# Attention stage of a one-core transformer block: VectorE takes the maximum of the new scores ahead of the low part of the turned tile

## What is computed

```python
q = rope(x @ w_q); k = rope(x @ w_k); v = x @ w_v            # 32, 8, 8 heads
lk = rope((x @ w_lq) @ w_lk); lv = x @ w_lv                  # 32 heads
attn = causal_softmax(q k^T / sqrt(128)) v                    # k, v repeated 4 times
lat  = causal_softmax(q lk^T / sqrt(128)) lv
x = layernorm(x + attn @ w_o + lat @ w_lo)
x = layernorm(x + top1_lora_ffn(x))                           # 8 experts of rank 16
```

## Time and profile before

| | us |
|---|---|
| median of 3 runs | 2026.87 |
| lowest, highest | 2025.49, 2027.67 |
| the profiled execution, its own time | 2023.68 |
| its span, first to last instruction | 2021.7 |
| TensorE busy in it | 1979.0 |
| VectorE busy in it | 1356.1 |
| ScalarE busy in it | 1054.6 |
| GpSimd busy in it | 1129.1 |

### The profile page before, as it was taken

The page is one execution under the profiler, slowest core; times in us unless marked ns, Lnnn a source line. Parts: engine busy times, 40 slices in busy tenths (PEclk is TensorE's granted clock), DMA queues, the critical chain, the costliest instruction groups (busy, mean ns, idle before and its releaser), DMA issues.

```text
span 2021.7 us, 39463 instructions
## 1 busy us (share of the span) xinstructions
PE 1979.0 (98%) x12640; PEld 1806.8 (89%) x12640; DVE 1356.1 (67%) x3356; ACT 1054.6 (52%) x2445; POOL 1129.1 (56%) x905
## 2 busy tenths in 40 slices
PE   7999999999999999999999999999999999999994
PEld 6989989899898989989899898999989899898993
DVE  6758667585775747758476675757757586675756
ACT  3746627375372745728356372654727366272641
POOL 6637476374664647556465664646566374763730
PEclk9999999999999999999999999999999999999997
DMA  5010010101000010000100001010010100100001
GB/s 177 12 35 1 23 36 12 35 1 43 15 22 24 2 57 1 22 24 3 55 1 22 24 22 36 1 45 1 23 36 12 35 1 23 36 13 21 2 12 42
DMA packets 19366, 50.85 MB, mean 25 GB/s; under 512 B 5824, under 2 KB 7872, under 8 KB 19008
## 3 DMA queue, kind: packets, MB, share of 16 engines
q1 hardware_dynamic: 18992, 45.90, 6.8%
q10 hardware_dynamic: 144, 2.10, 0.2%
HBM read 45.89 MB, written 2.10 MB: 24 GB/s over the span
## 4 chain that ended last, share of the span: by engine, by line
PE 97%; DVE 1%; issue 1%; POOL 0%; DVEq 0%; POOLq 0%; ACT 0%; ACTq 0%
PE ps L349 28%; PE ps L350 28%; PE ps L351 28%; PE ps L435 13%; DVE stats L845 0%; PE ps L529 0%; PE ps L544 0%; PE ps L521 0%; DVE acc L870 0%; POOL pt_lo L688 0%; DVE acc L908 0%; DVE stats L844 0%; POOL mask L678 0%; DVE neg_max L782 0%; DVE acc L831 0%
## 5 line engine op out<-in xcount | busy, mean ns | idle before, releaser
L712 POOL TENSOR_TENSOR probs<-probs,inv_sum 128x640 f32<-128x640 f32 (+7 forms) x512 | 582.9, 1150 | 343.9 <-DVE inv_sum L789 342.9
L782 DVE CUSTOM_DVE_ANT_0 probs<-ps,mask 128x640 f32<-128x640 f32 (+7 forms) x512 | 384.3, 753 | 167.2 <-PE ps L351 121.1
L724 DVE TENSOR_TENSOR pt_lo<-ps,pt_hi 128x512 fp32r<-128x512 f32 (+3 forms) x768 | 399.0, 547 | 75.1 <-ACT pt_hi L551 73.2
L551 ACT ACTIVATE pt_hi<-ps 128x512 fp32r<-128x512 f32 (+3 forms) x768 | 347.0, 487 | 164.0 <-PE ps L435 160.8
L580 ACT ACTIVATE probs<-probs,neg_max 128x640 f32<-128x640 f32 (+7 forms) x512 | 397.0, 776 | 60.5 <-DVE neg_max L782 49.3
L349 PE MATMUL ps<-pt_hi,val_hi 128*128 128x256 f32 x1216 | 353.8, 291 | 0.0
L350 PE MATMUL ps<-pt_lo,val_hi 128*128 128x256 f32 x1216 | 342.7, 282 | 0.0
L351 PE MATMUL ps<-pt_hi,val_lo 128*128 128x256 f32 x1216 | 342.5, 282 | 0.0
L435 PE MATMUL ps<-ident,probs 128*128 128x128 f32 x2304 | 334.4, 273 | 0.0
L703 POOL TENSOR_TENSOR probs<-probs 128x512 f32<-128x512 f32 x144 | 186.7, 1296 | 198.9 <-DVE probs L758 198.9
L435 PEld LDWEIGHTS ps<-ident,probs 128*128 128x128 f32 x2304 | 271.9, 140 | 23.6
(11 more groups left out here) (100 smaller groups left out, 4025.6 us busy)
## 6 DMA issues: line engine op xcount, KB each, us to landing
raw<-wo SPq DMA_DIRECT2D x32, 512.0 KB, 3.4
raw<-wq SPq DMA_DIRECT2D x16, 512.0 KB, 3.8
raw<-wlv SPq DMA_DIRECT2D x16, 512.0 KB, 3.6
raw<-wkv SPq DMA_DIRECT2D x8, 512.0 KB, 3.6
acc<-xT SPq DMA_DIRECT2D x4, 512.0 KB, 6.2
wlk_raw<-wlk SPq DMA_DIRECT2D x16, 128.0 KB, 3.0
acc<-x ACTq DMA_DIRECT2D x1, 2048.0 KB, 8.8
out<-acc SPq DMA_DIRECT2D x8, 256.0 KB, 2.4
```

Source lines behind the costliest of these rows:

```text
L551: return nc.scalar.activation(dst, src, ACT.Copy)
L712: nc.gpsimd.tensor_tensor(b, b, inv_sum[:, k % 8:k % 8 + 1].to_broadcast([P, b.shape[-1]]), ALU.mult).then_inc(q["normed"], 1)
L724: return nc.vector.tensor_tensor(dst, src, h, ALU.subtract)
L782: nc.vector.tensor_tensor_reduce(out=probs_of(n).rearrange("p (b n) -> p b n", b=b), in0=scores_of(n), in1=mask[:, S - w:S].rearrange("p ( ...
```

## The change

In the slot loop of VectorE's program two steps change places: `row_max` of tile k now comes ahead of `probs_lo` of tile k-5. Nothing else is changed.

```diff
                     for k in range(SLOTS):
+                        if EARLY + MID <= k < TILES:
+                            row_max(g, pair, k)
                         if 0 <= k - LO_LAG < TILES:
                             probs_lo(g, pair, k - LO_LAG)
-                        if EARLY + MID <= k < TILES:
-                            row_max(g, pair, k)
                         if EARLY <= k - 1 < TILES:
                             inverse(g, pair, k - 1)
```

## The result

The changed kernel takes 2109.4 us (median of 4 runs, 2106.1 to 2110.15) against 2026.4 (2025.49 to 2027.67): slower by 83 us, a ratio of 1.0406 with a 95% interval of 1.0388 to 1.0424. Forecast were 2117 and a range of 2080 to 2175. One run of the first experiment with four banks and the change took 2400.27 us at a granted clock of 0.788, and no figure here includes it.

A forecast was written before the change was run, and what follows sets the result against it. The prediction took TensorE, without idle time in the slots, to bound the kernel. Turn waits of 5.66 us a pair, times 16 = 91 us, on 2023.7 gave 2114, plus 3.2 for the median 2117; range 2080 to 2175.

The forecast's parts named there:

- TensorE has nothing to give back, the margin is what counts: In the slots TensorE is busy 60.57 of 60.60 us, so any wait is added in full, 16 times.
- The mechanism: TensorE's turns wait for banks held by later low parts: +91 us, 82 in 100.
- Slots 24 and 30: Even slots with long distances between turns: loss 0, at most 0.1 us.
- The sum, slot by slot: Turn waits in named slots add without growing: 5.66 us a pair, times 16 = 91 us.
- slots 22 and 23: Turns lose 0.18 us in slot 22 and 0.50 in slot 23, where VectorE is late after a short product.
- slots 31 and 32: At the pair's end, without scores between two turns, the second unit starts 1.38 us later.
- Earlier maxima gain nothing: TensorE's waits for maxima precede the exchanged steps: gain taken as 0, bounded by 8.7 us.
- Other work queued behind the maximum costs nothing: Reciprocals, even slots' maxima, SP's loads and GpSimd's weight parts keep their margins: cost 0.
- the flush after each VectorE operation: Two VectorE steps ahead of a turn each 0.4 us longer, over 9 places: sum 115 us higher; not adopted.
- The clock, the fourth rival: TensorE's clock falls to half for a quarter of the slots' 970 us: +242, 2360 us; 3 in 100.
- VectorE's idle time ahead of `pt_lo`: Sign in the profile after: this idle time on ScalarE nearly gone, that ahead of L782 up.
- busy times were to be unchanged: Sign in the profile after: the engines' busy times stay the same.

The follow-up runs named there:

- the first experiment with four banks and the change: Changed kernel with four PSUM banks for turned blocks and one for products: 2127.72 us, 74.4 over its control with the same banks.
- The two halves of the exchange: Against the kernel before, maximum first in odd slots only: 2095.85 us, +70.5; in even slots only: 2049.29 us, +23.9.
- one product bank: Four banks for turned blocks, one for products, against the kernel before: with the maximum first 2127.72 us, +101.7; without 2053.35 us, +27.4.
- the control with one product bank and the output's low part first: Kernel before with four turned banks, one product bank, output's low part first in VectorE's slot, low part before maximum: 2197.37 us, +171.
- The same kind of exchange: Kernel before, with tile 2's maximum ahead of the value unit's low part and reciprocals in a group's second pair: 2021.96 us, -4.0.
- The wait alone: Kernel before, with VectorE's wait for the scores of tile k placed ahead of the low part of tile k-5: 2047.95 us, +22.6.

## Why the prediction was right, and where it was off

**TensorE has nothing to give back, the margin is what counts.** Shown: the span grew by 86.3 us, and the new waits are 92.4 by the weight loads. Of the 86.3 some 2 are not of the change: the first turn of the first pair starts at 61.00 after 58.49, ahead of every exchanged step.

**The mechanism**: turns wait for `pt_lo`, 150 to 200 pieces, about 90 us, the longest 1.3. Measured 184, 92.4 and 1.2. The two halves of the exchange show that it comes from the slots named. Slots 24 and 30, for which 0 to 0.1 was forecast, have small waits (0.34 us at the weight load in slot 30), and by the starts they cost next to nothing.

**The sum, slot by slot.** The delay that each place adds is read from the starts of the same turn in both traces (after minus before, differences of successive ones). The first and the last, slots 7 and 33, in the kernel before and then in the changed one:

```profile
308.74 0.52 PE L435 MATMUL ps<-ident,probs 128*128 128x128 f32 x3
...
364.21 0.27 PE L435 MATMUL ps<-ident,probs 128*128 128x128 f32 x1
```

```profile
321.44 0.52 PE L435 MATMUL ps<-ident,probs 128*128 128x128 f32 x3
...
382.18 0.27 PE L435 MATMUL ps<-ident,probs 128*128 128x128 f32 x1
```

The distances are 12.70 and 17.97 us, so the pair grew by 5.27 us, 84 us over 16 pairs, where the forecast had 5.66 and 91. Within it:

| place | forecast, us | measured, us |
|---|---|---|
| slot 8 | 0.25 | 0.18 |
| slot 10 | 0.56 | 0.54 |
| slot 12 | 0.53 | 0.50 |
| slot 15 | 0.71 | 0.70 |
| slot 18 | 0.74 | 0.72 |
| slot 20 | 0.81 | 0.82 |
| slots 22 and 23 | 0.68 | 0.48 |
| slots 31 and 32 | 1.38 | 1.30 |
| all others | 0 | 0.03 |
| pair | 5.66 | 5.27 |

**The term that was most mis-sized** is slots 22 and 23, 0.20 of the 0.39 us by which the pair's sum is too high; slots 8 and 31 with 32 have 0.07 and 0.08 each. For slot 23 the forecast laid VectorE's steps from the first maximum to the low part of tile 17 end to end with their full durations. The rows of the changed kernel:

```profile
356.70 0.56 DVE L782 CUSTOM_DVE_ANT_0 probs<-ps,mask 128x384 f32<-128x384 f32 x1 [2.46 <-PE ps L351]
...
357.19 0.88 DVE L724 TENSOR_TENSOR pt_lo<-ps,pt_hi 128x512 fp32r<-128x512 f32 x2
...
358.38 0.95 DVE L782 CUSTOM_DVE_ANT_0 probs<-ps,mask 128x768 f32<-128x768 f32 x1
...
359.25 0.68 DVE L724 TENSOR_TENSOR pt_lo<-ps,pt_hi 128x512 fp32r<-128x512 f32 x1
```

The maximum printed with 0.56 is followed after 0.49 (by its accumulator read and the low part), that with 0.95 after 0.87. From the first maximum to the end of the low part of tile 17 it is 3.23 us (359.93 - 356.70); the forecast had 3.51 (344.03 - 340.52). That is 0.28 less, enough for the 0.20. An overlap of this kind, 0.07 to 0.08 a step, was in the forecast for two low parts in a row and was left out between the other steps.

**Earlier maxima gain nothing.** Right: the scores' waits for maxima are 8.7 us in both kernels.

**Other work queued behind the maximum costs nothing.** Right in this kernel: GpSimd waits longer for the reciprocals (417.6 us after 342.9), but the list of waits has no new one of TensorE for GpSimd or for the output's low part. How near that was is seen with one product bank, where the output's low part, at the end of the same queue, made 77.3 us of waits (26.3 without the change).

**The rules weighed.** By the flush after each VectorE operation, of which the Trainium skill tells ("VectorE: DVE Perf Modes", section on the DRAIN), the prediction had an estimate about 115 us higher. It left out that the same section goes on: a next operation that is not held starts earlier. The steps above follow one another 0.07 to 0.08 us *before* the printed end, so the rows agree with that sentence and not with the flush as a price, and so does the measured total. The clock, the fourth rival, did not fall. The changed kernel in the same pair's slots:

```profile
315.50:381.40 65.90, 63.15 (x456) 57.41 (x455) 48.17 (x142) 48.76 (x117) 39.13 (x33) 1.00 0.06 17
```

Some 12 waits of 0.2 to 1.2 us in 66 us leave the granted clock at 1.00, 2.4 GHz. The Trainium skill's account of a kernel that idles briefly and often and loses clock by it ("TensorE: Matmul & The Clock Gate", section on psum-queue depth-cycling) does not fit this kernel. Something of the kind shows only in the control with one product bank and the output's low part first, in six pairs of 16, behind waits of 0.63 and 1.36 us that stand close together.

**What was not foreseen in the signs**: VectorE's idle time ahead of `pt_lo` was to be nearly gone. It fell only from 75.1 to 59.6 us. In the stretch of slots from 315.5 to 381.4 no wait of `pt_lo` is left in the trace; the rest lies after the last maximum of each pair, where nothing was exchanged (1.53 and 2.07 us in this pair). And busy times were to be unchanged: TensorE's printed one rose by 41.0 us, as told above.

## What to carry to other kernels

In an engine's queue that runs in order, a step placed first takes everything behind it along into its wait. So before exchanging two steps, ask for each when its input exists and how far ahead of need its result is: here the low parts had their input early and 2 us of cover, the maximum's input came late and its result had slack, so the exchange spent the cover to buy slack. The same kind of exchange paid 4 us where the maximum's input came before that of the other step. And price it in the queue's starts, place by place: ten places in a pair, each under 1.4 us, made 4% of the kernel.

## What was unexpected of the hardware

What is put first does not cost in proportion. The wait alone ahead of every low part made 22.6 us, the wait with the maximum 83.0. In the odd slots the wait with the maximum made 70.5 us ahead of both units and 14.7 ahead of the second alone. A wait of TensorE is seen nearly whole only at the weight loads (92.4 us, for 84 of delay); the matmuls' rows show 41.3 of it. And waits of up to 1.2 us, some 12 in a pair, left the clock at 2.4 GHz, while two close together, 0.63 and 1.36 us, were followed by 1.2 GHz in six pairs of 16 of one control.
